# Residual added by VectorE onto turned rows, ScalarE's squares placed later in their step, and fewer fills in the setup

## The reference

```
mod = silu(c) @ wmod -> sa, ca, ga, sb, cb, gb per batch   (|ga|, |gb| at least 0.25)
h = layernorm(x) * (1 + ca) + sa
x = x + ga * attention(h)
h = layernorm(x) * (1 + cb) + sb
x = x + gb * experts(h)
```

## Time and profile before

| | |
|---|---|
| median of 3 runs | 1110.35 us (1106.92 to 1112.86) |
| profiled execution | 1111.9 us, of which the span is 1110.2 |
| busy in the span | PE 935.1, DVE 775.5, ACT 721.6, POOL 811.7 us |
| mean granted TensorE clock | 0.955 |
| setup, attention, experts | to 31, 31 to 863, 863 to the end |

### The profile page before, as it was taken

The page is one execution under the profiler, slowest core; times in us unless marked ns, Lnnn a source line. Parts: engine busy times, 40 slices in busy tenths (PEclk is TensorE's granted clock), DMA queues, the critical chain, the costliest instruction groups (busy, mean ns, idle before and its releaser), DMA issues. The chain is left out here.

```text
span 1110.2 us, 30824 instructions
## 1 busy us (share of the span) xinstructions
PE 935.1 (84%) x9473; PEld 742.2 (67%) x9473; DVE 775.5 (70%) x2067; ACT 721.6 (65%) x1612; POOL 811.7 (73%) x1352
## 2 busy tenths in 40 slices
PE   2346899889999899998999989998872799999967
PEld 2335677767777777777777777776652688888852
DVE  8576668777777777777777777777746466555536
ACT  2435678887778877888787887876562455555520
POOL 8366668888888888888888888887435366666644
PEclk9997999999999999999999999998985899999989
DMA  7336556565666656666566665655411353333339
GB/s 189 114 110 161 150 139 172 152 178 137 168 159 158 172 147 160 161 158 173 143 163 159 153 178 146 163 156 157 118 44 49 79 168 93 91 91 91 83 138 357
DMA packets 233854, 160.39 MB, mean 144 GB/s; under 512 B 57376, under 2 KB 220512, under 8 KB 233568
## 3 DMA queue, kind: packets, MB, share of 16 engines
q1 hardware_dynamic: 222416, 133.77, 46.0%
q0 software_dynamic: 8448, 17.45, 5.1%
q10 hardware_dynamic: 2832, 7.20, 1.7%
HBM read 81.38 MB, written 76.19 MB: 142 GB/s over the span
## 5 line engine op out<-in xcount | busy, mean ns | idle before, releaser
L919 DVE TENSOR_REDUCE peak<-pre 128x6 f32<-128x768 f32 x256 | 244.5, 955 | 116.4 <-PE pre L759 113.5
L1151 ACT ACTIVATE PT<-sc 128x768 f32<-128x768 f32 x256 | 204.6, 799 | 35.3 <-PE sc L746 32.9
L950 DVE TENSOR_TENSOR sc<-sc,decay 128x512 f32<-128x512 f32 x256 | 177.5, 693 | 30.4 <-PE sc L730 25.3
L1637 POOL DMA_INDIRECT yab<-y_out,xt x136 | 131.4, 966 | 82.8 <-issue 63.4
L1359 POOL DMA_INDIRECT xg<-stage,slot_i x128 | 130.9, 1022 | 62.9 <-issue 26.8
L759 PE MATMUL pre<-causal,identb 128*128 128x256 bf16 x512 | 144.7, 283 | 0.0
L758 PE MATMUL pre<-KT,queries 84*128 84x256 bf16 x512 | 143.5, 280 | 0.0
L757 PE MATMUL pre<-KT,queries 84*128 84x128 bf16 x512 | 116.5, 228 | 20.4 <-DMA queries<-line_rows 12.6
L1591 DVE TENSOR_TENSOR hid<-silu,up 128x256 f32<-128x256 f32 x136 | 57.3, 421 | 82.0 <-ACT silu L1545 82.0
L743 PE MATMUL sc<-queries,KT 99*128 99x128 bf16 x512 | 101.6, 223 | 13.2 <-issue 6.8
L1545 ACT ACTIVATE silu<-up 128x256 f32<-128x256 f32 x136 | 52.2, 384 | 88.4 <-PE up L1481 88.4
(11 more groups left out here) (279 smaller groups left out, 2731.9 us busy)
## 6 DMA issues: line engine op xcount, KB each, us to landing
line_rows<-line_part SPq DMA_DIRECT2D x64, 216.0 KB
dim_rows<-dim_part SPq DMA_DIRECT2D x64, 192.0 KB, 2.1
KT<-dim_rows SPq DMA_DIRECT2D x64, 192.0 KB
queries<-dim_rows SPq DMA_DIRECT2D x64, 192.0 KB
line_rows<-line_part SPq DMA_DIRECT2D x64, 144.0 KB
KI<-line_rows SPq DMA_DIRECT2D x64, 144.0 KB
QI<-line_rows SPq DMA_DIRECT2D x64, 144.0 KB
xt<-xg SPq DMA_DIRECT2D x136, 65.0 KB, 1.9
```

The source lines that it names most:

```text
L919: nc.vector.reduce_max(peak[half][:, i:i + 2, 0:3], pre[:, :, 0:3 * P].rearrange("p n (g k) -> p n g k", g=3), AX.X)\
L950: nc.vector.tensor_tensor(seeded(p), seeded(p), decay[:, 2 * p:2 * p + 2, :].unsqueeze(2).broadcast_to([P, 2, NT, P]), ALU.mult).then_inc( ...
L1151: nc.scalar.activation(PT[p % 4][:], sc[:, window], ACT.Exp).then_inc(exped.sem, 1)
L1637: nc.gpsimd.indirect_dma_start(yab, bass.IndirectOffsetOnAxis(xt[r][:, D:D + 1].bitcast(i32), 0), y_out[r % 8][:], None).then_inc(y_sent[r ...
```

## The change

Four edits in one. (1) The job `res` only turns yT by two transposes; VectorE adds the result to x_all in place and then takes the statistics; ScalarE's copy is gone. (2) ScalarE's square comes behind all copies of step p = 4. (3) The peak rows follow the line rows directly (`PEAK0` = 84, `TOP` = 87), so fewer rows have to be zero: VectorE fills one half of 84 rows of each QF, GpSimd sets 32 rows of each KT to one and then one half of 84 rows to zero. (4) The key mask is made at the start of GpSimd's setup and its copy KI moves from the end of VectorE's setup to near its start.

```
-PEAK0 = 96
+PEAK0 = DIMS + LINES
...
+        def pairs(tile):
+            return tile[:].rearrange("p h t -> p (h t)").bitcast(u32).rearrange("p (h t) -> p h t", h=H)
...   GpSimd, setup (the three key mask steps move up behind ident)
-                    step(nc.gpsimd.memset(v["KT"][m][64:96].rearrange("p h t -> p (h t)").bitcast(u32), 0))
-                    step(nc.gpsimd.memset(v["KT"][m][96:P].rearrange("p h t -> p (h t)").bitcast(u32), ones_pair))
+                    step(nc.gpsimd.memset(v["KT"][m][64:96].rearrange("p h t -> p (h t)").bitcast(u32), ones_pair))
+                    step(nc.gpsimd.memset(pairs(v["KT"][m])[0:PEAK0, :, P // 2:P], 0))
...   VectorE, setup
-                    nc.vector.memset(v["KT"][m][32:64].rearrange("p h t -> p (h t)").bitcast(u32), 0)
-                    nc.vector.memset(v["QF"][m][32:64].rearrange("p h t -> p (h t)").bitcast(u32), 0)
-                    nc.vector.memset(v["QF"][m][64:96].rearrange("p h t -> p (h t)").bitcast(u32), 0)
+                    nc.vector.memset(pairs(v["QF"][m])[0:PEAK0, :, 0:P // 2], 0)
...   behind az, ahead of the wait for the turned weights
+                dve.wait_ge(key_mask_ok, 1)
+                nc.vector.tensor_copy(v["KI"][0:MR].rearrange("p h (t k) -> p (h t) k", t=NT),
+                                      key_mask[1][:].unsqueeze(1).broadcast_to([MR, H * NT, P]))
...   and the same three lines removed behind the decay products
...   TensorE, job res
-                        settle(pe, pe_settled)
                         for t in range(NT):
                             blk = slice(t * P, (t + 1) * P)
-                            nc.tensor.matmul(B[:, blk], ident[:], x_all[:, span(jb * T + t * P, P)], start=True, stop=False)
-                            last = nc.tensor.matmul(B[:, blk], yT[:, blk], ident[:], start=False, stop=True)
+                            last = nc.tensor.transpose(B[:, blk], yT[:, blk], ident[:])
...   VectorE, p == 7
+                        wait(dve, ready["res"], jb)
+                        rows = x_all[:, span(jb * T, T)]
+                        nc.vector.tensor_tensor(rows, rows, bank[BANK["res"]][:, 0:T], ALU.add).then_inc(used["res"].sem, 1)
                         wait(dve, used["res"], jb)
...   ScalarE (res is also taken out of the list of jobs that it copies)
-                    elif name == "res":
-                        nc.scalar.activation(x_all[:, span(jb * T, T)], B[:, 0:T], ACT.Copy).then_inc(done, 1)
...
-                        if p == 4 and live(b + 3):
-                            squared(b + 3)
...   behind evacuate("norm2", b - 2, par)
+                        if p == 4 and live(b + 3):
+                            squared(b + 3)
```

More of the change, by code:

```diff
@@ L273, in _ @@
                                         pattern=[[-1, P]], channel_multiplier=1).then_inc(ident_ok, 1)
+                nc.gpsimd.memset(query_mask[0][:], MASK)
+                step(nc.gpsimd.memset(key_mask[0][:], 1.0))
+                nc.gpsimd.affine_select(out=key_mask[1][:], in_=key_mask[0][:], compare_op=ALU.is_ge, fill=0.0, base=-1,
+                                        pattern=[[1, P]], channel_multiplier=-2).then_inc(key_mask_ok, 1)
                 step(nc.gpsimd.iota(dist_i[:], pattern=[[1, P]], base=0, channel_multiplier=-1))
@@ L305, in _ @@
                 ones_pair = 0x3F803F80
[L306 to L309, removed]
                 step(nc.gpsimd.affine_select(out=query_mask[1][:], in_=query_mask[0][:], compare_op=ALU.is_ge, fill=0.0, base=0,
@@ L435, in _ @@
                 last.then_inc(arg_ok, 1)
-                dve.wait_ge(key_mask_ok, 1)
-                nc.vector.tensor_copy(v["KI"][0:MR].rearrange("p h (t k) -> p (h t) k", t=NT),
-                                      key_mask[1][:].unsqueeze(1).broadcast_to([MR, H * NT, P]))
                 dve.wait_ge(out_bias_ok, 1)
@@ L514, in attend @@
         used = {j: signal("used_" + j) for _, _, j, _, _ in JOBS}
-        sp_settled, dve_settled, pool_settled, act_settled, pe_settled, init = (
-            sem(n) for n in ("sp_settled", "dve_settled", "pool_settled", "act_settled", "pe_settled", "init"))
+        sp_settled, dve_settled, pool_settled, act_settled, init = (
+            sem(n) for n in ("sp_settled", "dve_settled", "pool_settled", "act_settled", "init"))
         stats, var, rstd, shift, normed = signal("stats", 2), signal("var"), signal("rstd"), signal("shift"), signal("normed")
@@ L1172, in body @@
                         for name, jb in [job for place in range(3) for job in jobs_at(b, p, place)]:
-                            if name[:-1] != "head" and name not in ("route", "rank", "norm2") and (name != "v" or b < 0):
+                            if name[:-1] != "head" and name not in ("route", "rank", "norm2", "res") and (name != "v" or b < 0):
                                 evacuate(name, jb, jb % 2)
```

## The result

The changed kernel takes 1133.26 us (median of 4 runs, 1130.43 to 1134.39) against 1109.1 before (4 runs): 1.021 of it, interval 1.0175 to 1.0246. It is slower, by 1.8 to 2.5%. The forecast was 1105 us, at the edge between faster and no change. The profiled execution took 1130.43 us, its span is 1128.6; the mean granted clock fell from 0.955 to 0.909.

A forecast was written before the change was run, and what follows sets the result against it. GpSimd's queue, not TensorE, was taken to pace the attention stage (22.92 us per period). Terms -2.2 + 3.9 - 2.1 - 2.5 - 2.2 = -5.1 us from the median 1110.35 gave 1105 us, range 1100 to 1112.

The forecast's parts named there:

- the term for the squares in the loop: Attention loop: square behind evacuations brings these 0.7 us earlier, VectorE's sum up to 0.6 us later; 0 per iteration.
- Disturbances: Attention loop: the clock dips behind 2.95 us of loss are absorbed by 1.2 us more slack; -2.5 us (0 to -3).
- Rival 3: Loop: TensorE idles before the turned lines, more clock dips, 0.7 us for each that gets through; 1121 us, chance 0.10.
- rival 1: Loop: TensorE paces it after all, GpSimd's fixed gap being a real wait; 24 us more gain, 1081 to 1090, chance 0.08.
- The early squares: Three iterations before the first scores: the moved square waits for hT and delays the chain; +3.9 us (2.5 to 4.3).
- The add on VectorE: Residual, each batch: a 128x256 add out of PSUM takes 0.43 us, absorbed by idle time; cost 0 in the loop.
- The setup's number: Setup: fewer fills and the moved KI copy end it earlier, -2.2 us; only 0.6 if KI holds GpSimd throughout.
- Where TensorE sets the pace: Batches 0 to 2 and the last residuals: cheaper residual transposes save time, -2.1 us and -2.2 us.
- Fewer rows in the scores: Score products with 87 instead of 99 rows: durations go by columns, so 0, within 0.02 us per product.

The follow-up runs named there:

- the run with the filled standstill: Changed kernel, but TensorE makes the four transposes of the first half of the heads three times into the same place; 1110.18 us, 0.9966 of before.
- the best version: Changed kernel with late sum, squares ahead of evacuations before the first scores, head transposes doubled in batches 3 to 26; 1104.78 us (0.9935), again 1103.09 (0.9919).
- the late sum: Changed kernel, but in the loop VectorE sums the squares after its next weighing of scores instead of ahead of it; 1110.64 us, 0.9978 of before.
- two other runs: Kernel before with only the square moved (99 rows), 1145.67 us; changed kernel with late sum and early squares put back (87 rows), 1106.53 us.

## Why the prediction was wrong

**The step that failed** is the term for the squares in the loop: "VectorE's sum of squares comes up to 0.6 us later, and the Newton steps on GpSimd after it; by the order of the queues they have about 1 us in hand. For GpSimd again nothing: 0 per iteration." The sum came 0.6 to 1.1 us later (3.0 to 3.5 instead of 2.4 us behind the start of GpSimd's cross products), and the Newton steps did have the time. But the working followed only the sum's consumer. Behind the sum in VectorE's own queue stand the weighing of the scores, a row maximum and the heads' division, and for these TensorE waits. This was asked for VectorE's add and not for the sum, which didn't move in its queue and only came to wait longer. In place of the 0 the runs showed two standstills of TensorE per period, of 1.0 and 0.6 us, dips of its clock behind them, and +18.0 us in the loop; with the square put back two dips of 6.8 us instead of nine were left among the 28 periods, and the loss was gone.

**Disturbances**, forecast as "absorbed", -2.5: with the sum of all periods at +18.0 instead of the -4.6 forecast for batches and disturbances, this is where the loss shows. The slack was really there: in the run with the filled standstill VectorE is as late and nothing is lost. What the term lacked is that the slack, taken in one place, makes the dips. With the standstill filled the 28 periods take 644.0 us instead of 647.0, -3.0; in the best version, which also has the late sum and the early squares back, 640.0 and 641.8.

**Rival 3** had the mechanism and the sign, at a chance of 0.10. Its place was wrong (before the turned lines; they do not appear among TensorE's waits), and its price too: 0.7 us is what a dip of 3.4 us costs before (periods of 23.57). After, a dip of 6.8 us costs 2.0 (periods of 24.9), and one of 3.4 with 99 rows 1.0. Not every period has one either: fourteen in 200 to 800 us, about every second period. The Trainium skill (TensorE: Matmul & The Clock Gate, HAM oscillation) was cited for it, with the remark that the few dips so far go against it; it is the section behind that one (the Trainium skill, TensorE: Matmul & The Clock Gate, A second HAM failure mode: psum-queue depth-cycling) that tells of small idle times between groups of matmuls which make the clock go down and up again. The trace after agrees with it: gaps of up to 1.2 and 0.6 us, and 14 dips in 600 us.

In rival 1 the sum is off by 5: 0.72 and 0.5 us in each of 24 periods make 29 us and not 24. Nothing hangs on it.

**What was right, and what was luck.** The early squares: +3.9 forecast; the distance from xhat to square grew from 0.77 by 1.15, 1.40 and 1.40, together 3.95, and putting them back brought the first line tokens 3.8 us forward. The add on VectorE: 0.43 estimated, 0.41 measured. GpSimd's period of 22.92 between the dips.

The setup's number came true, -2.2 forecast and 2.18 measured at the first xhat (1.6 to 2.5 in the other runs with these edits), but by another path, which is luck. KI did hold GpSimd, one cast of 0.19 us taking 2.17, and GpSimd's fills ended at 25.10 instead of 24.56; for that case the working had only 0.6. The gain came since ez was not held by the QI copy: it was done at 11.56, before that copy began (13.23), and VectorE reached the decay products at 20.17, beside the fills, instead of at 25.06 behind them.

Where TensorE sets the pace, -2.1 and -2.2 were forecast. The first three of the 28 periods take 68.9 instead of 71.0 us, and from the last line tokens on it is 347.9 instead of 350.1. The signs hold in the other runs on the average; single values scatter as much as the terms are large (350.1 to 355.3 us from the last line tokens on with the old residual, 347.1 to 351.7 with the new one as it stands), so the fit to a tenth is luck.

With the early squares as changed and most of the dips gone, the run with the filled standstill takes 0.9966 of before (0.9938 to 0.9993); the forecast's 1105 is 0.9952 of its median. The other terms together were thus about right; the squares in the loop were not.

**Fewer rows in the scores**, forecast as 0 by the durations of the products, may not be free: 5.4 us in one pair, and 4.8, not clear of the spread, in the other, both with longer dips. The durations are indeed the same 0.22 us; they say nothing of the dips. The cause stays open.

## What to carry to other kernels

When an operation moves back in one engine's queue, follow its result into the consumer's queue and list everything behind the consumer there, not only what uses the result. Idle time of an engine that isn't the bottleneck is not free on TensorE: look at how its standstills lie to one another before pooling them, since the clock that falls afterwards is paid while it has work. (That closeness counts is the reading of this case, not a tested rule.) Where a standstill can't be closed, a few useless transposes in it can cost less than the clock, and they also tell on the chip whether lateness or the clock is to blame.

## What the runs showed of the hardware

- The clock's dips in the loop come in two lengths here, 3.4 and 6.8 us, at half the full clock; in the places shown here they stand right behind standstills of TensorE of 0.6 to 1.2 us. The sum of its waits does not tell: from 250 to 710 us 43.7 us of waits went with ten dips, 44.2 with five, 35.9 (the kernel before) with four, and 40.8 with none (the best version's first run).
- In two pairs of kernels matmuls of 87 instead of 99 rows went with longer dips, although their durations are the same 0.22 us; two other runs go against a rule by rows, and the cause is open.
- Of two engines that hold each other in the setup, the one that had begun went on: KI on VectorE (5.70 to 7.98) stretched GpSimd's cast from 0.19 to 2.17 us, and GpSimd's QI copy (3.61 us from 13.23) held a small VectorE operation for 3.58 us.
